# Second layer's bound on the scores: the difference and the maximum as two row tiles, in groups of four in front of the bursts of the values' products

## What is computed

```python
q5 = (x @ Wq).reshape(b, t, H, E, DH)
kv = (x @ Wkv).reshape(b, t, 2, H, E, DH)
q = jnp.einsum('bthed,bthe->bhtd', q5, sd_g)
k = jnp.einsum('bthed,bthe->bhtd', k5, ss_g)
v = jnp.einsum('bthed,bthe->bhtd', v5, ss_g)
attn = jax.nn.softmax(jnp.einsum('bhid,bhjd->bhij', q * scale, k), axis=-1)
out = jnp.einsum('bhij,bhjd->bihd', attn, v)
```

## Time and profile before

| what | us |
|---|---|
| median of 3 runs | 1695.55 |
| lowest and highest | 1686.46, 1697.53 |
| the profiled execution's own time | 1687.58 |
| its span | 1685.8 |
| head 0 of the second layer (units 0 to 31) | 139.8 |
| each of heads 1 to 6 | 118.0 to 118.1 |
| head 7 | 93 |

### The profile page before, as it was taken

One profiled execution on the slowest core, in us unless ns is written; L12 is line 12 of the kernel. 1 busy time (PEld: TensorE's weight loads), 2 busy tenths in 40 slices (PEclk: granted clock), 3 DMA queues, 4 the chain that ended last, 5 costly groups with the idle time before them and its releaser, 6 DMA issues.

```text
span 1685.8 us, 27140 instructions
## 1 busy us (share of the span) xinstructions
PE 1556.2 (92%) x8404; PEld 1012.7 (60%) x8404; DVE 1254.2 (74%) x2518; ACT 939.7 (56%) x1582; POOL 847.9 (50%) x935
## 2 busy tenths in 40 slices
PE   4699999999999976689999999999999999999998
PEld 2455565565565545466666666567576666666555
DVE  3997787687679536777887778787778787777664
ACT  3446756756755631344655655655655656556652
POOL 2530000000001133458869879788689699698452
PEclk9599999999999987989999999999999999999998
DMA  2000000000000000000000000000000000000000
GB/s 64 0 1 1 2 1 2 1 1 1 1 1 1 1 12 13 1 1 13 0 13 1 1 13 2 0 13 1 13 1 1 13 1 1 1 1 1 1 7 19
DMA packets 12230, 9.39 MB, mean 6 GB/s; under 512 B 3840, under 2 KB 11584, under 8 KB 12096
## 3 DMA queue, kind: packets, MB, share of 16 engines
q1 hardware_dynamic: 12096, 7.66, 1.7%
HBM read 6.61 MB, written 1.05 MB: 5 GB/s over the span
## 4 chain that ended last, share of the span: by engine, by line
PE 63%; POOL 18%; DVE 9%; issue 4%; ACT 4%; SPq 1%; DMA 0%; DVEq 0%; ACTq 0%; POOLq 0%
PE ps L887 10%; PE ps L700 9%; PE ps L734 7%; PE ps L719 7%; PE ps L860 5%; PE ps L875 5%; POOL gs L1526 4%; PE ps L667 4%; PE ps L876 4%; POOL gsum L1527 3%; POOL z L572 3%; POOL onm L566 3%; PE ps L898 2%; POOL h_qk L1528 2%; DVE mxp L1201 2%
## 5 line engine op out<-in xcount | busy, mean ns | idle before, releaser
L1080 ACT ACTIVATE pbuf<-ps 128x512 f32<-128x512 f32 x512 | 301.6, 599 | 170.4 <-PE ps L876 166.2
L976 ACT ACTIVATE pbuf<-ps 128x1024 f32<-128x1024 f32 (+3 forms) x320 | 280.1, 897 | 182.5 <-PE ps L722 92.2
L1201 DVE TENSOR_REDUCE mxp<-ps 128x1 f32<-128x512 f32 (+2 forms) x432 | 279.1, 685 | 82.8 <-PE ps L700 51.4
L1407 DVE TENSOR_TENSOR den<-den,pbuf 128x1024 f32<-128x1024 f32 x224 | 312.8, 1396 | 1.9
L887 PE MATMUL ps<-pbuf,h_v 128*64 128x512 f32 x1024 | 248.7, 606 | 0.0
L1066 ACT ACTIVATE relu<-ps 128x512 f32<-128x512 f32 x256 | 152.2, 599 | 161.2 <-PE ps L860 132.1
L1359 DVE TENSOR_TENSOR gt<-ps,gate 128x320 f32<-128x320 f32 x384 | 181.6, 483 | 78.4 <-POOL h_v L1536 36.4
L700 PE MATMUL ps<-kM,qT 128*128 128x512 f32 (+3 forms) x640 | 230.9, 414 | 9.2 <-ACT kM L963 4.9
L875 PE MATMUL ps<-q1T,k1T 128*128 128x512 f32 x512 | 215.3, 421 | 11.4 <-ACT pbuf L1080 9.9
L1380 DVE CUSTOM_DVE_ANT_0 relu<-ps,relu 128x512 f32<-128x512 f32 x256 | 174.2, 684 | 64.5 <-PE ps L860 61.7
L719 PE MATMUL ps<-qT,kM 128*128 128x512 f32 (+3 forms) x640 | 199.5, 381 | 8.5 <-ACT pbuf L976 8.5
(11 more groups left out here) (224 smaller groups left out, 2799.5 us busy)
## 6 DMA issues: line engine op xcount, KB each, us to landing
wraw<-in_Wkv SPq DMA_DIRECT2D x16, 160.0 KB, 2.5
wraw<-in_Wq SPq DMA_DIRECT2D x8, 160.0 KB, 2.3
out<-x SPq DMA_DIRECT2D x4, 256.0 KB, 2.3
wqkv<-in_wqkvT SPq DMA_DIRECT2D x1, 192.0 KB, 3.9
masks<-in_masks SPq DMA_DIRECT2D x1, 128.0 KB, 4.1
dft<-in_dft SPq DMA_DIRECT2D x1, 128.0 KB, 2.3
wout<-in_Wo SPq DMA_DIRECT2D x2, 64.0 KB, 2.6
ident<-in_ident SPq DMA_DIRECT2D x1, 64.0 KB, 5.8
```

The source lines that it names most:

```text
L976: nc.scalar.activation(pbuf0[:, u % NP0, :, off:CH], ps[:, b:b + 2, off:CH], ACT.Exp, scale=float(D0) ** -0.5).then_inc(s_exp, 1)
L1080: nc.scalar.activation(pbuf1[:, u % NP1, i, :], ps[:, i, :], ACT.Exp, scale=float(D1) ** -0.5).then_inc(s_exp1, 1)
L1201: v.tensor_reduce(mxp[:, i, h:h + n, b], sc.rearrange("p (h k) -> p h k", h=n), AX.X, ALU.max).then_inc(s_read0d, 1)
L1407: v.tensor_tensor(dn, dn, w, ALU.add).then_inc(s_den1, 1)
```

## The change

The queries' high part moves from rows 0 to 63 of `q2T` to rows 64 to 127, and the shift with rows of zeros to rows 0 to 63; `k2T` has ones on rows 0 to 63 and the low part below. Then `dif` takes rows 0 to 63 of `q1T` and `kd`, and `max` takes rows 64 to 127 of `q2T` and `k1T`: each contracts 64 rows in place of 128, and they are placed at row tiles (0, 0) and (64, 0). The low part of the queries no longer enters the shift. Chunk 0 of head 0 stays as it was.

The steps also move. `dif`, `max`, `dif`, `max` of two tiles form a quad, four to a chunk, 124 in all for 31 chunks. In heads 1 to 7 all quads but two a head stand directly in front of a burst of `V`, after the unit's second `S` (units 1, 3, 5, 7 to 21 and 27, 29, 31 of a head); the quads for units 26 and 28 stand in the preparation, behind the unit's first `S`.

```diff
-            start = end - M1 if c > 1 else u - MAX1 + 0.4 if c else u - U1 + last + STAGE1[2] + 0.9
...
-            out += [(start + (end - start) * k / len(items), item) for k, item in enumerate(items)]
...
+def quads():
+
+    by_unit, others = {}, []
+    for h in range(H1):
+        for c in range(NC):
+            if h == 0 and c == 0:
+                continue
+            u = U1 * h + M1 * c
+            for k, p in enumerate(p for p in range(NC // 2) for _ in range(TPC // 2)):
+                pairs = [(h, TPC * c + 2 * (k % 2) + i, p) for i in range(2)]
+                quad = [(kind, *pair) for pair in pairs for kind in ("dif", "max")]
+                if (h, c) == (0, 1) or (h, c, k) == (0, 2, 0):
+                    others += [(5.05 + 0.38 * k if c == 1 else 8.0, step) for step in quad]
+                elif c or k % 2:
+                    by_unit[u + (2 * k - 9 if c else k - 6)] = quad
+                else:
+                    others += [(u + k - 6, step) for step in quad]
+    return by_unit, others
...
+            seq += QUADS.get(u, [])
             if 0 <= u - 2 < U1 * H1:
                 if u % 2:
                     seq += [("V", u - 3), ("V", u - 2)]
...
+                    if h or it >= TPC:
+                        at = (0, 0) if kind == "dif" else (D1, 0)
+                        rows = slice(at[0], at[0] + D1)
+                    queries = (q2T if at == (D1, 0) else q1T)[h % 2]
...
+                    pe.matmul(ps[:, bank, :], queries[rows, P * it:P * (it + 1)], keys,
+                              start=True, stop=True, tile_position=at).then_inc(s_turn1, 1)
...
-                    pe.matmul(ps[:, i, :], k2T[h % 2][0:D1 + 1, t], q2T[h % 2][0:D1 + 1, q],
+                    pe.matmul(ps[:, i, :], k2T[h % 2][:, t], q2T[h % 2][:, q],
...
-                    nc.scalar.activation(q2T[h % 2][D1:D1 + 1, CH * c:CH * (c + 1)],
-                                         ps[D1:D1 + 1, ring1.bank(step), :], ACT.Copy).then_inc(s_read1a, 1)
+                    nc.scalar.activation(q2T[h % 2][0:D1, CH * c:CH * (c + 1)],
+                                         ps[0:D1, ring1.bank(step), :], ACT.Copy).then_inc(s_read1a, 1)
```

More of the change, by code:

```diff
@@ L117, in preparation1 @@
 def preparation1():
-    out = first_head()
+    out = first_head() + quads()[1]
     for h in range(H1):
@@ L137, in preparation1 @@
                 continue
-            end = u + M1 * c - MAX1
-            start = end - M1 if c > 1 else u - MAX1 + 0.4 if c else u - U1 + last + STAGE1[2] + 0.9
[L140 to L148, removed]
-            out += [(start + (end - start) * k / len(items), item) for k, item in enumerate(items)]
+            end = u + M1 * c - MAX1 + (0.4 if (h, c) == (0, 1) else 0)
             out += [(end, ("m", h, c)), (end + 1.35, ("q2", h, c))]
     return sorted(out, key=lambda p: p[0])
+def quads():
[15 more added lines that the diff above has]
+    return by_unit, others
 def paced(preparation, units):
@@ L318, in build @@
         mx1 = s1("mx1", [P, TPC])
-        sk1 = s1("sk1", [P, TPC, P])
-        sk2 = s1("sk2", [P, TPC, D1])
+        sk = s1("sk", [P, TPC, 3 * D1])
         sq1 = s1("sq1", [P, TPC, P])
@@ L424, in foreground0 @@
             return seq
+        QUADS = quads()[0]
         def foreground1(u, half):
@@ L854, in _ @@
                     wait_read(pe, ring1, ("t", h, 2 * p + 1, 0))
+                    rows, at = slice(0, P), None
+                    if h or it >= TPC:
+                        at = (0, 0) if kind == "dif" else (D1, 0)
+                        rows = slice(at[0], at[0] + D1)
+                    queries = (q2T if at == (D1, 0) else q1T)[h % 2]
                     if kind == "dif":
                         pe.wait_ge(s_kd, NC // 2 * h + p + 1)
-                        keys = kd[:, p, :]
+                        keys = kd[rows, p, :]
                     else:
-                        keys = k1T[h % 2][:, CH * (2 * p + 1):CH * (2 * p + 2)]
-                    pe.matmul(ps[:, bank, :], q1T[h % 2][:, P * it:P * (it + 1)], keys,
-                              start=True, stop=True).then_inc(s_turn1, 1)
+                        keys = k1T[h % 2][rows, CH * (2 * p + 1):CH * (2 * p + 2)]
+                    pe.matmul(ps[:, bank, :], queries[rows, P * it:P * (it + 1)], keys,
+                              start=True, stop=True, tile_position=at).then_inc(s_turn1, 1)
                 elif kind == "q2":
@@ L1055, in _ @@
                         act.wait_ge(s_sc1, 2 * U1 * (h - 1))
-                    rows, q = slice(0, D1 if w == 1 else P), slice(CH * c, CH * (c + 1))
+                    rows, q = slice(D1 if w == 1 else 0, P), slice(CH * c, CH * (c + 1))
                     if w == 2:
-                        nc.scalar.activation(q2T[h % 2][0:D1, q], ps[0:D1, ring1.bank(step), :], ACT.Copy)
+                        nc.scalar.activation(q2T[h % 2][D1:P, q], ps[0:D1, ring1.bank(step), :], ACT.Copy)
                     nc.scalar.activation((k1T, k2T, q1T)[w][h % 2][rows, q],
```

10 lines of the change are left out of this document (5 added, 5 removed).

## The result

| what | before | after |
|---|---|---|
| median of 4 runs, us | 1695.91 | 1728.08 |
| lowest and highest | 1686.46, 1697.53 | 1723.14, 1736.73 |
| span of the profiled execution | 1685.8 | 1721.3 |
| ratio of the times, 95% interval | | 1.0207 [1.0151, 1.0262] |
| head 0 | 139.8 | 140.3 |

The change is slower by 2%, 47 us above the forecast and outside its range. The loss is in heads 1 to 6 alone: 34.1 of the 35.5 us of the spans.

The account below looks back on a forecast made before the run. PE's own work was taken as the bound, except where POOL ends last (46 of 118 us a head). 6 x -1.1 - 2 + 1 = -7.6, about -9 with small gains: 1679, written as 1681; range 1660 to 1708.

Parts of the forecast that it names:

- Unit price: A quad in front of a burst costs 0.65 us against 0.93 for four matmuls, saving 0.28.
- the forecast's estimate from it: From the skill's 3.07 times, a pair would be 0.30 and a quad would save 0.14 rather than 0.28; not used.
- The stage with projections: Heads 1 to 6: of ten quads four are kept, 4 x 0.28 = 1.1 us a head gained.
- The ring: PSUM banks: first reading of a `proj` behind a burst comes some 0.7 us later, covered by five turns, no cost.
- quads wait for banks: A quad takes four of five banks before the burst; 0.7 at 75 quads, 52 us against 9: 1730; chance 13%.
- POOL as the bound of six quads: Heads 1 to 6, units 5, 7, 9, 13, 15, 17: POOL ends last, PE only waits longer, nothing kept.
- The stage without projections: Heads 1 to 6: steps S lose their cover, other waits go; sum -0.1, taken as nothing, within 1 us a head.
- units 0 and 1: Stage without projections: no singles use the time while ACT's weight casts hold the second exponential back; +0.2 us.
- units 26 and 27: Stage without projections: two quads in place of six singles, 3.46 us becomes 4.05.
- units 28 and 29: Stage without projections: a wait of some 0.45 us from `relu` is avoided; -0.25 in all there.
- Heads 0 and 7: Head 0, same pattern behind unit 8, -2 us; head 7, without projections, +1 us.
- D behind the maxima at no cost: DVE at the burst: two `max` (0.76 each) go before `D`, using the 3.28 us DVE stood; no cost.

Follow-up runs that it names:

- `D` cut: DVE's sum of the exponentials cut to 128 of 1024 columns in seven of eight units: 0.9874 in the old order, 0.9870 in the new, to the kernel before.
- both cuts: `D` cut plus POOL's work for the experts' output cut to one column of 64: 0.9862 old order, 0.9864 new, to the kernel before.

## Why the prediction was wrong, step by step

- **Unit price:** right, 0.66 against 0.65, and the overlap of the tiles too. The sign named for it, pairs 0.23 apart and the burst 0.55 behind the first, is off by 0.10 each: the open load lies behind the first pair's start (0.33 to the second). The sum over a head holds as well: with every matmul at what it costs where nothing holds the next, PE's work in head 3 falls from 88.3 to 84.1 us, 4.2 for the 4.1 of the steps. Of that 2.1 are left in after, since three quads have a wait inside their second pair, which then no longer streams side by side (0.23 each), and waits under 0.2 us, not in the table, grow by 1.3. With `D` cut 3.5 are left. The Trainium skill has 3.07 times for four row tiles (TensorE: Matmul & The Clock Gate, Measured speedup vs the span model); the forecast's estimate from it, 0.79 for the quad, isn't borne out for these two tiles.
- **The stage with projections, the step that failed.** Forecast -1.1 us a head, measured +3.1 in head 3 (82.6 to 85.6). The step said that six quads of ten would keep nothing and four would be kept. The ring was dismissed in one clause, that the first reading comes 0.7 later "for which the ring has five turns". The quad itself takes four of the five, and its last product waits for all earlier ones but one, a sentence that stands in the text of a rival. The case against that rival (no `max` shortly before, readings grouped) looked at the wrong readers: it is the `proj` of the same unit that are unread, behind a `D` that takes 1.98 beside POOL's sums (1.41 in the earlier trace rows) and behind POOL itself.
- **Rival "quads wait for banks"**, given 13%, is what happened, and 1730 its time. That its time comes so near is luck. Its price was wrong in form: not 0.7 at each of 75 quads, but five waits in head 3 that sum to 4.7 us, 1.1 to 1.2 each at the three worst products; steps S and the clock, which it didn't have, make up the rest. The Trainium skill warns that packing speeds up the matmuls and not the emptying of PSUM (TensorEngine Tiling (Array Packing), PSUM Bottleneck). The late reading of banks is what these 4.7 us show, but not the speed of the tiles as its cause: the full array in the same order waits 4.4.
- **POOL as the bound of six quads.** "PE only waits longer for it: nothing kept" was right in that POOL's run isn't shorter (35.0 and 34.9 us into the head), but it took nothing kept for the worst case. Before, PE's wait there lay in front of a `proj` or a transpose, with the burst already issued; now the burst waits with it, and units 8 and 9 take 9.4 us for 7.5.
- **The stage without projections:** forecast -0.1 for all, measured +0.5 in units 22 to 31 and +0.35 in units 0 and 1, together within the 1 us given. The -0.1 leaves out units 30 and 31, to which its own price would give +0.2 (measured +0.35). Inside it two signs were wrong: units 26 and 27 gained 0.3 (forecast a loss of 0.6), units 28 and 29 lost 0.9 (forecast a gain of 0.25).
- **Heads 0 and 7:** +0.5 and +0.4 for -2 and +1; small.
- **D behind the maxima at no cost:** right in effect, though not for the reason given, as the kernel with `D` ahead of the quad shows (1.0195 against 1.0207).
- **A term that wasn't in the sum:** stretches at half the clock. Against head 3 the other five heads are longer by 10.9 us in all. That and 6 x 3.9 is 34.3, of the 34.1 measured for these heads.

What stays open: how the 3.3 us of quad waits that go with `D` cut part between DVE's own time and the stretched POOL; and what decides which heads get a half-clock stretch.

## What to carry to other kernels

When work that shares a ring of buffers is grouped, count the ring: a group of n in a ring of n + 1 waits, at its last member, for every earlier user but one, and whatever is queued behind the group waits as well. Work that is spread between two waiting steps does a second job there; price it before it is taken out (here 2.2 us a head, of the 3.5 to 4.2 that the tiles save). And a stretch in which another engine ends last isn't neutral ground for the bound engine: ask what stands in the queue behind the place where the wait will now be.

## What the runs showed of the hardware

**Behind long waits in front of a burst the clock was halved, in some heads.** In unit 9 of head 3 and of head 5 the third and fourth product wait as long. Timeline of PE in head 5 of after:

```profile
1388.01 0.49 PE L876 MATMUL ps<-kd,q1T 64*128 64x512 f32 x1 [0.95 <-DVE gt L1375]
1389.46 0.79 PE L876 MATMUL ps<-k1T,q2T 64*128 64x512 f32 x1 [0.95 <-DVE gt L1375]
1390.18 3.68 PE L903 MATMUL ps<-pbuf,h_v 128*64 128x512 f32 x8
1393.79 0.64 PE L853 MATMUL ps<-wh,xh 128*128 128x320 f32 x1
```

```profile
1389.40:1395.80 6.40, 6.34 (x15) 2.87 (x16) 5.16 (x10) 0.60 (x1) 3.30 (x6) 0.50 0.01 1
```

The granted clock in this stretch is 0.50, the 1.2 GHz level of the two, and the burst takes 3.61 us instead of 1.87. From the fourth product to the next transposes it is 6.7 us, in head 3, which had the same waits and kept 2.4 GHz (1.00), 3.7. That 3.0 is the whole difference between the two heads (124.9 and 121.9). Five of heads 1 to 6 in after have such a stretch, all in unit 9, four of them shorter (heads 1.6 to 2.4 us longer than head 3). None has one in the kernel before, and none with `D` cut except one head with both cuts. Two heads have one in the new order with the full array, so the tiles aren't needed for it. The fourth product starts 2.9 us after the first pair, and in head 5 this delay was followed by a loss of 3.0 more. That the waits bring the half clock is inferred from where the stretches lie; what decides that one head gets it and another doesn't stays open.

**A drain is cheap, a lone tile isn't.** Entering and leaving the tiled mode costs 0.09 and 0.10 us, but around single products, 64 in a head and few of them side by side, it adds 0.38 where it was measured (1.08 for 0.70), and the head grew by 14.8 us with 3.4 us fewer waits than before.
